# Counting edges with one-hot matrices: two comparisons of 128 columns become one instruction of 256 columns

## The reference

```
agg = x + jax.ops.segment_sum(x[src], tgt, num_segments=n)      # convolution
comb = dst * num_rel + edge_type                                # relations
cnt = jax.ops.segment_sum(jnp.ones(src.shape), comb, num_segments=num_nodes * num_rel)
```

## Time and profile before

| | |
|---|---|
| median of 3 runs | 5740.71 us (5737.53 to 5747.76) |
| profiled execution | 5738.76 us |
| its span in the profile | 5736.5 us |
| VectorE busy | 3804.2 us (66% of the span) |
| first tile of the stage to its last, VectorE | 60.05 to 729.3 us |
| tiles in the stage | 800 fixed and 227 further |

### The profile page before, as it was taken

How to read it: one execution, slowest core, us unless ns; L and a number is a source line. 1 busy time by engine, 2 the same in 40 slices (tenths; PEclk the granted TensorE clock), 3 DMA queues, 4 the chain that set the end, 5 groups by cost and what they waited for, 6 DMA issues and landing times. The chain is left out here.

```text
span 5736.5 us, 107111 instructions
## 1 busy us (share of the span) xinstructions
PE 3956.4 (69%) x31282; PEld 2987.8 (52%) x31283; DVE 3804.2 (66%) x9916; ACT 2218.3 (39%) x2892; POOL 1395.5 (24%) x1703
## 2 busy tenths in 40 slices
PE   4667676825445444545456888888888879997997
PEld 2222266824444444444444444444444449995996
DVE  7999967755556555565633555544555568886887
ACT  2433433011111111111112555555555547874885
POOL 0000000017777777777771000000000000000000
PEclk8999988955555555555556999988999969996998
DMA  1111144722222222222111111101111121112110
GB/s 38 68 57 61 65 149 158 277 49 56 64 59 59 54 59 59 64 59 60 47 50 40 58 57 57 57 30 64 57 57 57 51 65 41 51 34 71 51 46 29
DMA packets 235223, 370.66 MB, mean 65 GB/s; under 512 B 169839, under 2 KB 175973, under 8 KB 235142
## 3 DMA queue, kind: packets, MB, share of 16 engines
q1 hardware_dynamic: 190006, 264.11, 14.2%
q0 software_dynamic: 41536, 85.08, 5.6%
q10 hardware_dynamic: 3600, 20.48, 0.9%
HBM read 292.58 MB, written 76.99 MB: 64 GB/s over the span
## 5 line engine op out<-in xcount | busy, mean ns | idle before, releaser
L1069 POOL DMA_INDIRECT en_got<-edge_q,en_now x1296 | 1302.0, 1005 | 408.9 <-issue 325.9
L1258 PE MATMUL en_t<-ident,en_got 128*128 128x128 f32 x1296 | 361.1, 434 | 957.3 <-DVE en_got L1152 957.3
L1296 ACT ACTIVATE en_hid<-en_t 128x512 f32<-128x512 f32 x324 | 193.4, 597 | 1648.9 <-DMA en_got<-edge_q,en_now 1402.7
L1258 PEld LDWEIGHTS en_t<-ident,en_got 128*128 128x128 f32 x1296 | 231.5, 217 | 1035.7 <-DVE en_got L1152 1035.7
L1266 PEld LDWEIGHTS en_o<-en_w2s,en_hid 128*128 128x128 f32 x2592 | 582.8, 333 | 0.0
L1266 PE MATMUL en_o<-en_w2s,en_hid 128*128 128x64 f32 x2592 | 577.4, 411 | 0.0
L1152 DVE TENSOR_TENSOR en_got<-en_got,p (+1 forms) x324 | 224.5, 693 | 494.2 <-ACTq L1290 461.4
L456 PE MATMUL cnt_ps<-cnt_hot_l,cnt_hot_k 128*128 128x400 bf16 x1600 | 358.6, 355 | 192.8 <-DVE cnt_hot_l L421 179.0
L1849 PE MATMUL r1s_ps<-hp,r1s_bits 128*128 128x193 bf16 x5000 | 423.5, 248 | 26.6 <-DVE r1s_bits L1802 13.6
L1849 PE MATMUL r0s_ps<-hp,r0s_bits 128*128 128x193 bf16 x5000 | 423.5, 248 | 26.7 <-DVE r0s_bits L1802 13.6
L1849 PEld LDWEIGHTS r1s_ps<-hp,r1s_bits 128*128 128x128 bf16 x5000 | 418.1, 98 | 32.0 <-issue 31.6
(11 more groups left out here) (393 smaller groups left out, 7619.5 us busy)
## 6 DMA issues: line engine op xcount, KB each, us to landing
en_got<-edge_q,en_now POOLq DMA_INDIRECT x1296
count_panels<-cnt_panel SPq DMA_DIRECT2D x25, 800.0 KB, 3.4
type_panels<-cnt_panel SPq DMA_DIRECT2D x25, 800.0 KB, 4.8
c0s_panel<-count_panels SPq DMA_DIRECT2D x25, 800.0 KB, 4.4
count_rows<-c0s_rows ACTq DMA_DIRECT2D x25, 800.0 KB, 3.5
c1s_panel<-count_panels SPq DMA_DIRECT2D x25, 800.0 KB, 5.7
c1s_rows<-count_rows SPq DMA_DIRECT2D x25, 800.0 KB, 7.3
en_raw<-count_panels SPq DMA_DIRECT2D x25, 800.0 KB
```

Source lines behind the costliest of these rows:

```text
L1069: pool.indirect_dma_start(out=got[:, i, j, :], out_offset=None, in_=k.q[:, :], in_offset=bass.IndirectOffsetOnAxis(ap=now[i][:, j:j + 1], ...
L1258: last = pe.transpose(tps[i % 2][:, j * P:(j + 1) * P], got[:, i, j, :], k.ident[:, :])
L1296: act.activation(hid[i % 2][:, :], tps[i % 2][:, :], ACT.Relu).then_inc(lined, 1)
```

## The change

The two comparisons of a tile become one instruction. Its first input is `here`, read twice by a step of 0 (2 x 128 columns). It is compared with the key of the row, and the result is multiplied by the second input: two factors per row, 1.0 and the power of two, each read 128 times by a step of 0. The output is the 256 columns of both keys, which already lay side by side. To have the two factors next to each other, `keys` and `now` get a fourth number per edge, the constant 1.0, which is written once ahead of the loop. The instruction for `lows` stays as it is, and so do all waits, TensorE's products and the buffers of the one-hot matrices.

```diff
-        keys = sb("keys", [P, NT, 3], F32)
+        keys = sb("keys", [P, NT, 4], F32)
-        now = [sb(f"now{u}", [P, FIX, 3], F32) for u in range(SETS)]
+        now = [sb(f"now{u}", [P, FIX, 4], F32) for u in range(SETS)]
...
-            own.do(v.tensor_copy(keys[:, :, 2], power[:, :].bitcast(F32)))
+            own.did(v.memset(keys[:, :, 2], 1.0))
+            own.do(v.tensor_copy(keys[:, :, 3], power[:, :].bitcast(F32)))
...
-            def tile(k2, lows, u, low_at, key_at, power_at):
-                v.tensor_scalar(k2[0], here[u][:, :], key_at, None, ALU.is_equal)
-                v.tensor_scalar(k2[1], here[u][:, :], key_at, power_at, ALU.is_equal, ALU.mult)
+            def tile(both, lows, u, low_at, key_at, factors):
+
+                v.scalar_tensor_tensor(both, here[u][:, :].unsqueeze(1).broadcast_to([P, 2, P]), key_at,
+                                       factors.unsqueeze(2).broadcast_to([P, 2, P]), ALU.is_equal, ALU.mult)
                 return v.tensor_scalar(lows, iota_l[:, :], low_at, None, ALU.is_equal)
...
-                    last = tile([hot_k[:, u % 2, j, c, :] for c in range(2)], hot_l[:, u % 2, j, :], u,
-                                *(now[u][:, j, c:c + 1] for c in range(3)))
+                    last = tile(hot_k[:, u % 2, j, :, :], hot_l[:, u % 2, j, :], u,
+                                now[u][:, j, 0:1], now[u][:, j, 1:2], now[u][:, j, 2:4])
...
-                        tile([more_k[:, ds(slot, 1), c, :].rearrange("p a n -> p (a n)") for c in range(2)],
+                        tile(more_k[:, ds(slot, 1), :, :].rearrange("p a c n -> p (a c) n"),
                              more_l[:, ds(slot, 1), :].rearrange("p a n -> p (a n)"), u,
-                             *(keys[:, ds(t, 1), c] for c in range(3))).then_inc(more_hots, 1)
+                             keys[:, ds(t, 1), 0], keys[:, ds(t, 1), 1],
+                             keys[:, ds(t, 1), 2:4].rearrange("p a c -> p (a c)")).then_inc(more_hots, 1)
```

## The result

The changed kernel takes 5756.32 us (median of 9 runs, 5753.0 to 5763.83) against 5742.43 us for the kernel before in the same series (9 runs, 5737.53 to 5754.02). The ratio is 1.0022, with a 95% interval of 1.0012 to 1.0032. That is 13.9 us slower, where 12.3 us were forecast. The sum came out well partly by luck: the changed stage itself lost 8.8 us in the profiles, less than forecast, and 5.5 to 7.4 us more were lost in a later stage that the forecast took to stand still.

A forecast was written before the change was run, and what follows sets the result against it. VectorE was taken to set the counts' stage. Longer tiles (+14.4 us), the memset (+0.9) and shrinking waits (-3.0) gave +12.3 us, so a median of 5753.0 us, slower by 0.21%, range 5738 to 5772.

The forecast's parts named there:

- The bound: Counts' stage, 58 to 732 us: VectorE sets it, busy 191.3 of 200 us; gains or losses reach the end in full.
- The pitch: Each tile's comparisons, start to start: 401 ns fused against 387 ns, +14 ns for 1027 tiles, +14.4 us.
- The gaps: VectorE's waits for ScalarE and TensorE between tiles: shrink a little as tiles get longer, -3.0 us.
- Ahead of the loop: Before the first tile: the memset of ones adds 0.9 us; writing with a step of four numbers adds nothing.
- The later stages: After the counts' stage: nothing moves; the stage's loss goes to the end in full.
- the prediction's own last sentence: Wrong altogether if the stage's length changed by something outside VectorE's row, or if a later stage moved.
- the bound of 0.2%: Whole kernel: about 0.2% (11.5 us) is what a measurement can tell from no change.
- The free value: Rival, fused instruction: the value per row costs nothing, pitch 339 ns, tile 48 ns less, 5692 us; chance 0.04.
- the slow stream: Rival, fused instruction: steps of 0 or mixed types slow it to 1.34 ns per column, 5834 us; chance 0.06.
- the half rate: Rival, fused instruction: 256 columns at 2.1 ns, +285 ns per tile, 6035 us; chance 0.04.
- The absorbed loss: Rival, waits before tiles: slower tiles only fill VectorE's waits, 5739 us, or 5729 if TensorE's go too; chance 0.18.

The follow-up runs named there:

- stt_128: Kernel before, with only the weighted comparison made by the new kind of instruction, over 128 columns; 33 us slower in the median, pitch 262 ns.
- early_before: Kernel before, with ScalarE laying out windows earlier (u + 3 behind an odd u, first four at the start); 17 us faster, 14.3 us of gaps left.
- early_after: Changed kernel with the same earlier layouts by ScalarE; 25 us faster than the changed kernel, 5.5 us of gaps left.
- same_places: Changed kernel plus 23 one-column memsets on VectorE ahead of its first tile, giving back the earlier count of 3395 instructions; ratio 1.0012.
- no_value: Changed kernel, fused instruction comparing with a constant instead of the row's key; pitch 335 ns, one execution of 14255.37 us with other data in later loops.

## Why the prediction was right, and where it wasn't

- *The bound.* VectorE sets the stage in both kernels, busy for 190.9 us of the stretch 200 to 400 us (191.3 before). Right, and `stt_128` shows it from the other side: a longer comparison goes to the end.
- *The pitch.* Forecast 401 against 387 ns, measured 396 against 386. The mechanism was right, as `stt_128` shows: a fixed part is saved (191 ns, where the prediction has 130 to 190), and 1.05 ns per column are paid. The term was mis-sized by a third (+10.3 us and not +14.4), since a difference of two large numbers takes an error of 5 ns in one of them in full.
- *The gaps.* Forecast -3 us, measured -3.9 (-6.5 in the second pair of profiles; the idle time, which the prediction named, fell by 2.1 and 3.7). That the size came out well is luck. 13.3 of the 33.3 us were the sequencer's slow loads, which the prediction didn't name, and in the changed kernel these fell to 2.2 us. The gaps that end with a layout of ScalarE, which it expected to shrink, grew from 20.0 to 27.1 us. That they hang on the chain through TensorE is shown: moving the layouts removed them in `early_before` and `early_after`, and in `stt_128` both kinds shrank, as the prediction has it. That they grew here because the time saved at the loads was waited for again at the next layout is my reading, which no run isolates.
- *Ahead of the loop.* Forecast 0.9 us, measured 2.5. I put the step of four numbers at nothing, and it cost about 0.9; the idling of 0.8 us before the memset was not in the sum at all. Line 411's own 1.34 ns per column, with a step of three, said that a step costs here, and I used that row only as a bound on something else. Of line 1811 I had misread the step of 0: its value is repeated for 192 columns and not 64, which changes nothing in the sum.
- *The later stages.* Forecast unmoved, measured 5.5 and 7.4 us slower in the edge maxima (two pairs of profiles). This is the step that failed, by the prediction's own last sentence. `same_places` puts it on the place of VectorE's code. Without it the change would cost 8.8 us, 0.15%, and `same_places` measures about that much (1.0012, with 1.0003 to 1.0021). That is under the bound of 0.2% that I had set: the direction was right, but "slower by 0.21%" owes its success to luck, a cause that I hadn't seen.
- *The rivals.* The free value, the slow stream and the half rate are excluded by 480 ns and 396 ns, and `no_value` shows what the free value would have given: 335 ns, near the 339 of line 303. The Trainium skill's rule of half rate for two sources that are not bf16 ("Vector Engine (DVE) Microarchitecture Reference", section "Points that are easy to get wrong") does not show here: with int16 and float32 sources, and with int16 on both, a column takes 1.05 ns, where the prediction's price for the half rate is 2.1. No run has bf16 sources, so whether those would be faster stays open. The absorbed loss is excluded as such (27 to 29 us of gaps remain), though gaps do take a quarter of a longer tile's time in `stt_128`.

## What to carry to other kernels

Fusing two short instructions saves a fixed part, and pays if the fused form streams about as fast as the two did. Here the two streamed a column in about 0.26 ns (an estimate from 233 ns for 400 columns and 163 for 128) and the fused one takes 1.05. So 191 ns of fixed part were saved (386 less 67 for the 256 columns, against 128), and 201 were paid (256 columns at 1.05 ns, less the 67). Before a wait is put down to an engine, look at what that engine's or the waiting engine's sequencer did in the two microseconds or so before it. And when a part of a program that nobody edited becomes slower, compare the packets of the instruction queues before looking for a story in the data.

## What was not expected of the hardware

- A register load from SBUF that VectorE's sequencer begins 0.2 to 1.7 us behind the issue of a panel's store of 800 KB takes 1.5 to 1.8 us instead of 0.6. ScalarE's loads show it too: 24 of 99 at about 1.77 us in the kernel before, begun 1.3 to 2.7 us behind a store, and none in the four kernels with early layouts, where they begin 0.9 us before one. That the store itself slows them is read from these starts; no run takes the store away.
- 23 instructions fewer in VectorE's program, far ahead of a loop, raised the fetched packets of one instruction queue from 42 to 147 and made the first six rounds of the edge maxima 13.6 us long instead of 12.1. 23 memsets of one column each, put where VectorE waits anyway, undid both.
- A value per row costs 61 ns of pitch in this kind of instruction (396 against 335 ns, at 256 columns).
- Writing float32 numbers with a step of four costs 1.76 us for 896 columns from int32 sums, 1.35 with a step of three and 1.09 side by side.
